# Window attention: the next image's score search interleaved with the second head group, its row transpose moved behind the q/k projection, and the division by the softmax sums cut in eight

## The chip, the cores and the metric

The kernel runs on one core of a Trainium2 chip. The metric is the device time of one execution, in microseconds (us); lower is better. Engine names are those of the profile: PE is TensorE (PEld its weight loads), DVE VectorE, ACT ScalarE, POOL GpSimd, SP the engine that issues the transfers.

## What is computed

Sixteen images of 192 channels and 32 x 32 pixels pass through a convolution layer, an attention layer and two state-space layers. The change touches the attention layer alone. Each pixel of each of 6 heads attends to the 7 x 7 window around it:

```python
qkv = jnp.einsum('bcij,oc->boij', x, w_qkv) + b_qkv[None, :, None, None]
q = qkv[:, :C] * scale
k = qkv[:, C:2 * C]
v = qkv[:, 2 * C:]
kp = jnp.pad(k, ((0, 0), (0, 0), (p, p), (p, p)))
...
for idx in range(win * win):
    dy, dx = (idx // win, idx % win)
    ks = kp[:, :, dy:dy + H, dx:dx + W].reshape(B, heads, dph, H, W)
    scores.append(jnp.einsum('bhdij,bhdij->bhij', qh, ks))
```

A softmax over the 49 positions, the weighted sum of v, an output projection and the residual follow. Keys outside the image are zero but count in the softmax (the "padding terms").

## The kernel before, in words

`attention` (from L1316) handles one image per turn of `main(n)`; the images run in pairs, with images 0 and 1 and the last two written out and a hardware loop of six turns over the pairs between. Turn n finishes image n and prepares image n+1. Each engine has its own `main(n)`, an instruction list in fixed order, and the engines meet only at semaphores.

On PE turn n is: `project` (q, k in three fills, v in four, all of image n+1), `project_out` (output of image n-1, two fills), `pass_b(n, 0)` (scores, then values and sums, of heads 0 to 2 of image n, in 12 pairs of units), `pass_a(n)` (24 pairs of units of image n+1's scores, computed only to find their row maxima), `norm` (group averages for image n+2), `pass_b(n, 1)` (heads 3 to 5), `to_row_layout` (transposes the maxima and padding terms of image n+1, which are then stored to DRAM and loaded back as rows).

All of these but the value sums write to one PSUM tile `work` of two buffers, used strictly in turn: fill k waits until fill k-2 has been drained. A class `Use` counts the fills (59 a turn) and gives each its buffer and number. Who drains: ACT takes q and k (`take_qk`, L1735 and L1737), the rows (`take_rows`, L1777) and the probabilities (`exps`, L1752); DVE takes v (`take_v`, L1853), the maxima (`maxima`, L1872), the averages (`norm_finish`, L1833) and the output (`residual`, L1932).

After each head group ACT copies the sums out (`keep_acc`, L1763 and L1765), and DVE's `divide` takes the reciprocal of the denominators (L1921) and multiplies (L1923). For group 0 of image n that stands on DVE behind the search, for group 1 at the start of turn n+1, ahead of `take_v`. POOL makes the low parts of q and k (`split`, L1995 and L2000). SP stores the three bf16 parts of q and k to DRAM and loads them back in another layout (`move_parts`), stores the output (`store`), and moves the rows (`move_rows`), in this order and waiting for each.

DVE's order in turn n: divide(n-1, 1), take_v, residual, copy_stacks 0, norm_stats, copy_stacks 1, maxima, norm_finish, divide(n, 0), split_padding. `copy_stacks` must be done, and the third q/k part loaded, before the search starts.

Of the kernel before, what the change touches and what calls it, by code (L numbers as in the profile page):

```python
# [10 lines left out]
ALU = mybir.AluOpType  # L11
# [1278 lines left out]
UNIT_PAIRS = 12  # L1290
MASK_ROWS = slice(64, 112)
A_FILLS = 59
# [23 lines left out]
def attention(nc, tag, x_src, x_dst, w, consts, batches):  # L1316
    L, HALF = 1024, 512
    ctx = ExitStack()
    with ctx:
# [93 lines left out]
        def project_use(n, j):  # L1413
            return Use(ZERO, 1 + j) if n is None else Use(n, (34 if n.first else 32) + j)

        def a_use(n, i):
            return Use(ZERO, 8 + i) if n is None else Use(n, 53 + i)

        def norm_use(n):
            return Use(ZERO, 0) if n == "start" else Use(ZERO, 32) if n is None else Use(n, 77)  # L1420

        def rows_use(n):
            return Use(ZERO, 33) if n is None else Use(n, 90 if has(n, 2) else 89)
# [6 lines left out]
        def b_use(n, g, i):  # L1430
            if not has(n, 1):
                return Use(n, (33, 45)[g] + i)
            return Use(n, (41, 78 if has(n, 2) else 77)[g] + i)
# [50 lines left out]
        with nc.Block() as block:  # L1484
            @block.sync
            def _(sp):
# [16 lines left out]
                def move_parts(n):  # L1503
# [3 lines left out]
                    for part, (t, made, k_made, places) in enumerate((  # L1507
                            (qk1, high_made, 3, ((0, q_a, q), (0, k_a, k))),
                            (qk2, mid_made, 1, ((64, q_a, q), (32, k_a, k))),
                            (qk3, low_made, 3, ((32, q_b, q), (0, k_b, k))))):  # L1510
                        if n is not None:
# [3 lines left out]
                        sp.wait_ge(part_stored[part], m.count(16, 16))  # L1515
                        if part == 0 and n is not None and not n.first:

                            sp.wait_ge(group_done, before(n).count(2, 2))
# [5 lines left out]
                def move_rows(n):  # L1524

                    m = after(n)

                    await_all(sp, [(rows_made, m.count(1, 1))] + ([(rows_loaded, m.count(32, 0)), (group_done, m.count(2, 0))]
                                                                  if n is not None else []))
# [13 lines left out]
                def prologue():  # L1543
                    load_residual(ZERO)
                    sp.wait_ge(xn_made, 1)
                    load(Batch(0, 1))
                    move_parts(None)
                    move_rows(None)

                def main(n):  # L1550
# [3 lines left out]
                    if has(n, 1):  # L1554
                        move_parts(n)
# [3 lines left out]
                    if has(n, 1):  # L1559
                        move_rows(n)  # L1560
# [4 lines left out]
            def _(pe):  # L1565
# [8 lines left out]
                def project(n):  # L1574
                    m = after(n)
                    pe.wait_ge(xn_made, m.count(1, 1))
                    for j in range(3):
# [7 lines left out]
                        last.then_inc(filled, 1)  # L1585
                    for j in range(4):
# [25 lines left out]
                def pass_a(n):  # L1612
# [5 lines left out]
                    for i in range(2 * UNIT_PAIRS):  # L1618
                        scores(a_use(n, i), m, i // UNIT_PAIRS, i % UNIT_PAIRS, q_a, q_b, k_a, k_b, 112)

# [20 lines left out]
                def pass_b(n, g):  # L1641
# [6 lines left out]
                    for half in range(2):  # L1648
# [4 lines left out]
                                         skip_group_check=True)  # L1653
                    for i in range(UNIT_PAIRS + 1):
                        if i < UNIT_PAIRS:
                            scores(b_use(n, g, i), n, g, i, k_a, k_b, q_a, q_b, 114)
                        if i:
                            values(n, g, i - 1)
                    nc.tensor.matmul(acc_den[:, 0:1], den_sel[:, 2, :], pad_rows[:, 0:1], start=False, stop=True,
                                     skip_group_check=True).then_inc(group_done, 1)  # L1660
# [5 lines left out]
                def project_out(n_next):  # L1666
                    pe.wait_ge(att_made, n_next.count(2, 0))
# [11 lines left out]
                def to_row_layout(n):  # L1679
                    f = rows_use(n)  # L1680
                    await_unit(pe, f)
                    pe.wait_ge(max_step, after(n).count(5, 5))
# [5 lines left out]
                def prologue():  # L1688
                    norm("start")
                    project(None)  # L1690
                    pass_a(None)
                    norm(None)
                    to_row_layout(None)

                def main(n):
                    if has(n, 1):
                        project(n)
# [16 lines left out]
            def _(act):  # L1714
                def normalise(m):
                    act.wait_ge(norm_step, m.count(7, 7))
                    if not m.first:
                        f = project_use(None if is_static(m, 1) else before(before(m)), 6)
                        await_fill(act, f)
                    for c in range(2):  # L1720
                        last = nc.scalar.activation(image(xn[:, c, :]), x[:, c, :].rearrange("p (y s x) -> p s y x", s=2, x=TILE_W), ACT.Identity,
                                                    scale=rstd[:, c:c + 1], bias=shift[:, c:c + 1])
                    last.then_inc(xn_made, 1)
# [33 lines left out]
                def keep_acc(n, g):  # L1757
# [3 lines left out]
                    if not (n.first and g == 0):  # L1761
                        act.wait_ge(att_made, n.count(2, g))
# [9 lines left out]
                def take_rows(n):  # L1772
                    f = rows_use(n)
                    await_fill(act, f)
                    if n is not None:
                        act.wait_ge(rows_stored, after(n).count(32, 0))
                    nc.scalar.activation(rows_bf[:, :, :], work[0:120, f.unit, :, 0:128], ACT.Copy).then_inc(rows_made, 1)  # L1777
                    act.wait_ge(rows_made, after(n).count(1, 1))
                    act.sem_inc(drained[f.unit], 1)

                def prologue():
                    normalise(ZERO)
# [3 lines left out]
                    normalise(Batch(0, 1))  # L1786
                    take_rows(None)
# [364 lines left out]
```

## Time and profile before

| what | value |
|---|---|
| time, median of 3 runs | 4305.36 us (4305.03 to 4306.83) |
| profiled execution: span from first to last instruction | 4308.6 us |
| profiled execution: device time of its own | not listed beside the span |
| attention layer in the profile | about 380 to 1710 us |
| mean granted TensorE clock | 0.952 |

The profile gives no device time for the profiled execution, so its span stands in for it. The span is 3.2 us (0.08%) above the median of the three timed runs.

In a timeline row the columns are start (us), length (us), engine, line, operation, tiles, count, and in brackets the idle time ahead of it with what ended it.

### The profile page before, as it was taken

Reading aid. Unit: us, or ns where it says so; the run is one execution under the profiler, and the core shown is the slowest. Engines: PE = TensorE matmul, PEld = TensorE weight load, DVE = VectorE, ACT = ScalarE, POOL = GpSimd, SP = SyncE. Lnnn points to the kernel's source line nnn. Section 1 sums busy time; section 2 is a strip of 40 time slices with the busy share of each in tenths; the row PEclk is TensorE's granted clock in tenths of the full one; section 3 lists DMA queues with packets and bytes.
Section 4 is the critical chain, followed back from the end, with each engine's and each line's share of the span. In section 5 each row is a group of like instructions: output and inputs, shape, how many; then the busy total and the mean of one; then the engine's idle time right before and its main releaser. Section 6 shows DMA issues by size and latency. Waiting matters only on the chain.

```text
span 4308.6 us, 119610 instructions
## 1 busy us (share of the span) xinstructions
PE 3710.7 (86%) x49136; PEld 2266.0 (53%) x49136; DVE 3432.3 (80%) x3492; ACT 2105.8 (49%) x2803; POOL 2659.4 (62%) x973
## 2 busy tenths in 40 slices
PE   4994899899999996789889888899898888888897
PEld 4994666666666664344444444444444444444443
DVE  6564567667576663699998998999999989999997
ACT  2331343444444443556555555555565555555563
POOL 1111121111211210599899999999999999999998
PEclk9997899999999998799999999999999999999999
DMA  9624142242332330553543543544535535435433
GB/s 101 85 44 108 54 124 81 85 119 70 95 109 69 105 91 25 120 116 79 125 106 83 125 102 92 125 94 103 122 84 120 112 79 124 109 79 130 103 87 83
DMA packets 296948, 416.40 MB, mean 97 GB/s; under 512 B 31369, under 2 KB 185741, under 8 KB 296385
## 3 DMA queue, kind: packets, MB, share of 16 engines
q1 hardware_dynamic: 295440, 408.35, 41.7%
q8 instruction: 412, 6.75, 0.7%
q14 instruction: 118, 0.97, 0.1%
q10 hardware_dynamic: 978, 0.34, 0.0%
HBM read 267.09 MB, written 91.16 MB: 83 GB/s over the span
## 4 chain that ended last, share of the span: by engine, by line
PE 27%; DVE 16%; issue 12%; ACT 3%; POOL 1%; DVEq 1%; DMA 0%; ACTq 0%; POOLq 0%
DVE ssm_h L1136 11%; PE ssm_u_ps L818 10%; PE ssm_y_ps L831 10%; PE ssm_scratch L848 4%; DVE ssm_b_diag L1160 3%; PE ssm_scratch L858 1%; DVE ssm_stats L1143 1%; POOL ssm_h L1216 1%; ACT ssm_decay L967 1%; PE ssm_u_ps L893 1%; DVE ssm_y_sb L1165 1%; ACT ssm_xn L994 1%; PE ssm_scratch L873 1%; PE ssm_scratch L867 0%; DVEq L1128 0%
## 5 line engine op out<-in xcount | busy, mean ns | idle before, releaser
L1216 POOL TENSOR_TENSOR ssm_h<-ssm_h,ssm_c_rep 128x2048 f32<-128x2048 f32 x384 | 1745.4, 4550 | 107.3 <-DVE ssm_h L1136 99.6
L967 ACT ACTIVATE ssm_decay<-ssm_delta_rep,ssm_a_neg 128x1024 f32<-128x1024 f32 x768 | 863.7, 1145 | 592.1 <-DVE ssm_h L1136 589.3
L818 PE MATMUL ssm_u_ps<-ssm_b_diag,ssm_dx_t 64*64 64x128 f32 x24576 | 865.7, 282 | 262.3 <-DVE ssm_h L1136 182.6
L818 PEld LDWEIGHTS ssm_u_ps<-ssm_b_diag,ssm_dx_t 64*64 64x64 f32 x24576 | 696.3, 137 | 698.9 <-issue 694.6
L1136 DVE TENSOR_TENSOR_SCAN ssm_h<-ssm_decay,ssm_h,ssm_u_ps 128x512 f32<-128x512 f32 x768 | 944.3, 1257 | 132.5 <-PE ssm_u_ps L818 131.4
L1136 DVE TENSOR_TENSOR_SCAN ssm_h<-ssm_decay,ssm_u_ps 128x512 f32<-128x512 f32 x768 | 887.2, 1195 | 35.8 <-ACT ssm_decay L967 16.9
L831 PE MATMUL ssm_y_ps<-ssm_h,ssm_state_sum 128*64 128x512 f32 x3072 | 798.1, 643 | 8.0 <-POOL ssm_h L1216 8.0
L1752 ACT ACTIVATE l_probs<-l_work 128x532 f32<-128x532 f32 (+1 forms) x384 | 217.6, 567 | 560.7 <-PE l_work L1606 554.0
L1160 DVE TENSOR_TENSOR ssm_b_diag<-ssm_b_t,ssm_lane 128x2048 f32<-128x2048 f32 x128 | 454.0, 3549 | 22.7 <-ACT ssm_b_t L1022 22.7
L2004 POOL TENSOR_TENSOR l_rstd<-l_var_eps,l_minus_half 96x2 f32<-96x2 f32 x16 | 11.1, 695 | 586.6 <-DVE l_var_eps L1841 586.6
L831 PEld LDWEIGHTS ssm_y_ps<-ssm_h,ssm_state_sum 128*64 128x64 f32 x3072 | 196.8, 144 | 326.3 <-issue 311.9
L1921 DVE RECIPROCAL l_den<-l_den 96x1024 f32<-96x1024 f32 x32 | 209.6, 6549 | 196.7 <-ACT l_den L1765 196.7
L1995 POOL TENSOR_TENSOR l_qk<-l_qk 128x1024 f32<-128x1024 f32 x48 | 111.6, 2325 | 398.4 <-ACT l_qk L1737 398.4
L1637 PE MATMUL l_acc<-l_probs,l_v 128*32 128x176 f32 (+3 forms) x3072 | 292.8, 275 | 24.5 <-ACT l_probs L1752 20.1
L1637 PE MATMUL l_acc_den<-l_probs,l_ones 128*32 128x176 f32 (+3 forms) x3072 | 291.1, 275 | 0.0
L1236 POOL TENSOR_TENSOR ssm_dx<-ssm_x_kept,ssm_delta 128x256 f32<-128x256 f32 x192 | 254.2, 1343 | 48.7 <-PE ssm_scratch L873 40.1
L1872 DVE TENSOR_REDUCE l_m_raw<-l_work 128x2 f32<-128x532 f32 (+1 forms) x384 | 238.0, 650 | 55.1 <-PE l_work L1606 48.9
L1606 PE MATMUL l_work<-l_k_a,l_q_a 128*128 128x176 bf16 (+3 forms) x1536 | 227.5, 223 | 60.4 <-DVE l_k_a L1863 29.7
L1226 POOL TENSOR_TENSOR ssm_delta<-ssm_relu,ssm_delta 128x512 f32<-128x512 f32 x96 | 249.0, 2594 | 22.7 <-ACT ssm_delta L1009 22.7
L1606 PE MATMUL l_work<-l_q_a,l_k_a 128*128 128x176 bf16 (+3 forms) x1536 | 238.6, 224 | 5.9 <-DVE l_g_mom L1833 5.9
L1637 PEld LDWEIGHTS l_acc<-l_probs,l_v 128*32 128x32 f32 x3072 | 189.6, 111 | 82.7 <-ACT l_probs L1752 30.8
L848 PE MATMUL ssm_scratch<-ssm_xn,ssm_w_delta 97*64 97x512 f32 x768 | 192.7, 624 | 31.7 <-issue 25.8
(163 smaller groups left out, 5554.7 us busy)
## 6 DMA issues: line engine op xcount, KB each, us to landing
ssm_c_rep<-ssm_c_by_state SPq DMA_DIRECT2D x256, 512.0 KB, 6.5
ssm_delta_rep<-ssm_delta SPq DMA_DIRECT2D x384, 128.0 KB, 5.9
l_qk_parts<-l_qk SPq DMA_DIRECT2D x48, 768.0 KB, 4.8
ssm_x<-x_after_l SPq DMA_DIRECT2D x32, 768.0 KB, 5.8
ssm_x_res<-x_after_l SPq DMA_DIRECT2D x192, 128.0 KB, 4.3
l_x<-x SPq DMA_DIRECT2D x64, 192.0 KB, 9.1
x_after_l<-l_x SPq DMA_DIRECT2D x64, 192.0 KB, 4.1
l_x<-x_after_l SPq DMA_DIRECT2D x16, 768.0 KB, 5.5
```

What stands on the lines that cost most here:

```text
L818: made = nc.tensor.matmul(u_ps[64 * par:64 * par + 64, ring("u", w), r, at:at + 128], dx_t[rows, db, 2 * win + k, 64 * g:64 * g + 64], b_d ...
L831: last = nc.tensor.matmul(y_ps[64 * g:64 * g + 64, :], state_sum[:, :], of_half(h[:, s % S_RING, npi, :], g), start=(npq == 0 and npi == 0 ...
L848: last = nc.tensor.matmul(scratch[64 * g:64 * g + 64, :], wt[n.layer][:, ci, 64 * db:64 * db + 64], xn[:, ci, g, :], start=(ci == 0), stop ...
L967: nc.scalar.activation(decay[:, 2 * (s % 2) + npi, :], delta_rep[:, db, :], ACT.Exp, scale=a_neg[:, n.layer, col:col + 1]).then_inc(decay_ ...
L1136: nc.vector.tensor_tensor_scan(h[:, s % S_RING, npi, t], decay[:, 2 * (s % 2) + npi, t], u, start, ALU.mult, ALU.add).then_inc(scanned, 1)
L1160: nc.vector.tensor_tensor(b_diag[:, npq].rearrange("p c a (j i) -> p (c a) j i", i=2), b, m, ALU.mult).then_inc(diag_made, 1)
L1216: nc.gpsimd.tensor_tensor(view, view, c_rep[:, 2 * q:2 * q + 2, :], ALU.mult).then_inc(c_applied, 1)
L1226: nc.gpsimd.tensor_tensor(delta[:, db, :], relu[:, :], delta[:, db, :], ALU.add).then_inc(delta_made, 1)
L1236: made = nc.gpsimd.tensor_tensor(by_lane(dx[:, :], w), in_order(x_kept[:, :], w), in_order(delta[:, db, :], w), ALU.mult)
L1606: last = nc.tensor.matmul(out[:, 0:own] if part == 0 else out[:, own:size], on[m.s][0:r, head, tile_at(TILES[ti])], off[m.s][0:r, head, 51 ...
L1637: last = nc.tensor.matmul(out, by, p, start=False, stop=(i == UNIT_PAIRS - 1), skip_group_check=True)
L1872: nc.vector.tensor_reduce(m_raw[:, 2 * i:2 * i + 2], work[:, f.unit, :, 0:size], AX.X, ALU.max).then_inc(drained[f.unit], 1)
```

## The change

The search fills of image n+1 are put between the score fills of head group 1 of image n on PE, in a list `MIXED`: 8 search fills first, then after each of the 12 group-1 fills one or two more until 24 are done. The averages for image n+2 come before them. On DVE, `maxima` comes after `norm_finish`, and the division of group 0 is cut into eight parts of 128 columns, one after each of the search fills 10 to 17. The division of group 1 is also in eight parts. `norm_stats` moves ahead of `residual`. On ACT the normalisation of image n+2 is split over two places (after exponentials 3 and 7), and the padding terms come after the last exponential. The row transpose of image n+1 moves from the end of turn n to turn n+1, between the q/k and the v projection; ACT takes the rows after q and k; SP moves them after q/k part 0 and ahead of parts 1 and 2.

```diff
+FIRST_SCORES = 8
+MIXED = [("a", i) for i in range(FIRST_SCORES)]
+for _i in range(UNIT_PAIRS):
+    _done = sum(kind == "a" for kind, _ in MIXED)
+    MIXED += [("b", _i)] + [("a", _done + k) for k in range(min(1 + _i % 2, 2 * UNIT_PAIRS - _done))]
+MIXED += [("a", i) for i in range(sum(kind == "a" for kind, _ in MIXED), 2 * UNIT_PAIRS)]
+PARTS = 8
+DIVIDE_AFTER = list(range(10, 10 + PARTS))
...
         def project_use(n, j):
-            return Use(ZERO, 1 + j) if n is None else Use(n, (34 if n.first else 32) + j)
+            return Use(ZERO, 1 + j) if n is None else Use(n, (34 if n.first else 31 if j < 3 else 32) + j)
...
-        def rows_use(n):
-            return Use(ZERO, 33) if n is None else Use(n, 90 if has(n, 2) else 89)
+        def rows_use(m):
+            return Use(ZERO, 33) if m.first else Use(m, 34 if has(m, 1) else 30)
...
# SP, main(n)
                     if has(n, 1):
-                        move_parts(n)
+                        move_parts(n, (0,))
+                    if not n.first:
+                        move_rows(n)
+                    if has(n, 1):
+                        move_parts(n, (1, 2))
                     if not n.first:
                         store(n)
                         load_residual(n)
-                    if has(n, 1):
-                        move_rows(n)
...
# PE
+                def pass_a_and_b(n):
+
+                    await_stacks(n)
+                    for kind, i in MIXED:
+                        if kind == "a":
+                            scores_a(n, i)
+                        else:
+                            if i == 0:
+                                start_group(n, 1)
+                            scores_b(n, 1, i)
+                            if i:
+                                values(n, 1, i - 1)
+                    values(n, 1, UNIT_PAIRS - 1)
+                    end_group()
...
                 def main(n):
                     if has(n, 1):
-                        project(n)
+                        project_qk(n)
+                    if not n.first:
+                        to_row_layout(n)
+                    if has(n, 1):
+                        project_v(n)
                     if not n.first:
                         project_out(n)
                     pass_b(n, 0)
-                    if has(n, 1):
-                        pass_a(n)
                     if has(n, 2):
                         norm(n)
-                    pass_b(n, 1)
                     if has(n, 1):
-                        to_row_layout(n)
+                        pass_a_and_b(n)
+                    else:
+                        pass_b(n, 1)
...
# ACT, main(n)
                     if has(n, 1):
                         take_qk(n)
+                    if not n.first:
+                        take_rows(n)
+                    if has(n, 1):
                         middle_part(n)
...
                         exps(n, 1, i)
-                        if i == 3 and has(n, 1):
-                            padding_terms(n)
-                        if i == 7 and has(n, 2):
-                            normalise(Batch(n.it + 1, n.s))
+                        if i in (3, 7) and has(n, 2):
+                            normalise(Batch(n.it + 1, n.s), i // 4)
+                    if has(n, 1):
+                        padding_terms(n)
                     keep_acc(n, 1)
-                    if has(n, 1):
-                        take_rows(n)
...
# DVE
+                def divide_part(n, g, part):
+                    if part == 0:
+                        dve.wait_ge(acc_kept, n.count(2, g + 1))
+                    cols = slice(part * L // PARTS, (part + 1) * L // PARTS)
+                    nc.vector.reciprocal(den[:, cols], den[:, cols]).then_inc(den_inverted, 1)
+                    dve.wait_ge(den_inverted, n.count(2 * PARTS, PARTS * g + part + 1))
+                    nc.vector.tensor_tensor(att[:, g, cols], att[:, g, cols], den[:, cols], ALU.mult).then_inc(att_made, 1)
...
                         take_v(n)
+                    if has(n, 2):
+                        norm_stats(Batch(n.it + 1, n.s))
                     if not n.first:
                         residual(n)
                     if has(n, 1):
                         copy_stacks(n, 0)
-                    if has(n, 2):
-                        norm_stats(Batch(n.it + 1, n.s))
-                    if has(n, 1):
                         copy_stacks(n, 1)
-                        maxima(n)
                     if has(n, 2):
                         norm_finish(norm_use(n), Batch(n.it + 1, n.s))
-                    divide(n, 0)
                     if has(n, 1):
+                        maxima(n)
                         split_padding(n)
+                    else:
+                        divide(n, 0)
```

## Rows read from the trace of the kernel before

**Rows 1.** The page: span, and busy time of each engine.
```profile
span 4308.6 us, 119610 instructions
```
**Rows 2.** Busy time by stage of one loop turn: start:end, length, busy (count), clock.
```profile
core 0: us, PE busy (x) PEld busy (x) DVE busy (x) ACT busy (x) POOL busy (x), PEclk, DMA share, GB/s
1162.60:1187.80 25.20, 23.26 (x75) 12.37 (x75) 11.41 (x8) 14.12 (x12) 13.28 (x6) 1.00 0.46 132
1187.80:1204.20 16.40, 16.26 (x295) 12.76 (x294) 15.01 (x16) 6.82 (x12) 0.47 (x1) 1.00 0.72 205
1204.20:1240.60 36.40, 32.19 (x488) 26.35 (x487) 25.58 (x47) 13.38 (x19) 0.69 (x1) 0.95 0.06 18
1240.60:1269.20 28.60, 25.00 (x76) 13.09 (x77) 13.32 (x8) 14.12 (x12) 12.24 (x6) 0.94 0.41 117
...
```
**Rows 3.** Who waited for whom, 757.7 to 1550.3 us, ten turns.
```profile
PEld l_work L1606 <- DVE l_m_raw L1872: 31.1, 110, 0.4
```
**Rows 4.** Timeline of PE, first tail.
```profile
1167.34 7.13 PE L1582 MATMUL l_work<-l_xn,l_w_qk 96*128 96x512 f32 x16 [0.85 <-ACTq L1779]
1174.31 1.46 PE L1591 MATMUL l_work<-l_w_v,l_xn 96*128 96x192 f32 x8
1176.87 4.17 PE L1591 MATMUL l_work<-l_w_v,l_xn 96*128 96x192 f32 x24 [1.09 <-ACT l_qk L1737]
1180.87 7.03 PE L1673 MATMUL l_work<-l_att,l_w_o 96*96 96x512 f32 x16
```
**Rows 5.** Timeline of ACT, first tail: the third q/k fill's second copy.
```profile
1175.62 1.20 ACT L1737 ACTIVATE l_qk<-l_work,l_qk_bias,l_qk_scale 128x1024 f32<-128x1024 f32 x1
```
**Rows 6.** Timeline of DVE, first tail.
```profile
1166.87 6.55 DVE L1921 RECIPROCAL l_den<-l_den 96x1024 f32<-96x1024 f32 x1 [10.09 <-ACT l_den L1765]
1173.45 1.22 DVE L1923 TENSOR_TENSOR l_att<-l_att,l_den 96x1024 f32<-96x1024 f32 x1
1175.81 0.56 DVE L1853 TENSOR_TENSOR l_v<-l_work,l_b_v 128x384 f32<-128x384 f32 x1 [1.14 <-PE l_work L1591]
```
**Rows 7.** Timelines of PE, POOL and DVE, second tail.
```profile
1243.57 12.26 PE L1582 MATMUL l_work<-l_xn,l_w_qk 96*128 96x512 f32 x24 [2.51 <-issue]
...
1251.38 2.12 POOL L1995 TENSOR_TENSOR l_qk<-l_qk 128x1024 f32<-128x1024 f32 x1 [26.97 <-ACT l_qk L1737]
...
1251.45 3.13 DVE L1923 TENSOR_TENSOR l_att<-l_att,l_den 96x1024 f32<-96x1024 f32 x1
```
**Rows 8.** Timeline of PE: first matmuls of two following search fills.
```profile
1204.19 0.25 PE L1606 MATMUL l_work<-l_k_a,l_q_a 128*128 128x176 bf16 x1
...
1204.62 0.24 PE L1606 MATMUL l_work<-l_k_a,l_q_a 128*128 128x176 bf16 x1
```
**Rows 9.** Timeline of DVE: search, and the end of norm_finish.
```profile
1204.81 1.09 DVE L1872 TENSOR_REDUCE l_m_raw<-l_work 128x2 f32<-128x418 f32 x2 [1.52 <-PE l_work L1606]
...
1211.70 5.15 DVE L1872 TENSOR_REDUCE l_m_raw<-l_work 128x2 f32<-128x532 f32 x8 [0.16 <-PE l_work L1606]
...
1224.52 0.16 DVE L1843 SCALAR_TENSOR_TENSOR l_shift<-l_g_mom,l_rstd 96x2 f32<-96x2 f32 x1 [0.88 <-POOL l_rstd L2004]
```
**Rows 10.** Timeline of PE, group 1: its longest wait.
```profile
1235.86 0.38 PE L1637 MATMUL l_acc<-l_probs,l_v 128*32 128x224 f32 x1 [1.41 <-ACT l_probs L1752]
```
**Rows 11.** Two stretches on either side of the start of group 1.
```profile
1220.10:1223.50 3.40, 2.69 (x29) 1.81 (x27) 3.03 (x16) 0.52 (x1) 0.00 (x0) 1.00 0.00 0
1223.50:1226.90 3.40, 3.40 (x52) 2.80 (x50) 2.52 (x3) 1.04 (x2) 0.69 (x1) 0.50 0.00 0
```
**Rows 12.** Timeline of SP's queue, first tail: issues.
```profile
1167.62 1.54 SPq L1531 DMA_DIRECT2D l_max_rows<-l_rows_bf  x2
1170.58 0.26 SPq L1535 DMA_DIRECT2D l_q_b<-l_max_rows  x1
...
1175.74 0.39 SPq L1514 DMA_DIRECT2D l_qk_parts<-l_qk  x1
1179.35 0.80 SPq L1522 DMA_DIRECT2D l_q_a<-l_qk_parts  x2
```

More of the change, by code:

```diff
@@ L1432, in b_use @@
                 return Use(n, (33, 45)[g] + i)
[L1433 removed]
+            return Use(n, 41 + i) if g == 0 else mixed_use(n, "b", i)
         def await_unit(pe, f):
@@ L1510, in move_parts @@
                             (qk3, low_made, 3, ((32, q_b, q), (0, k_b, k))))):
+                        if part not in which:
+                            continue
                         if n is not None:
@@ L1514, in move_parts @@
                         sp.dma_start(qk_dram[part].rearrange("(t p) c -> p t c", p=128), t[:, :, :]).then_inc(part_stored[part], 16)
-                        sp.wait_ge(part_stored[part], m.count(16, 16))
-                        if part == 0 and n is not None and not n.first:
-                            sp.wait_ge(group_done, before(n).count(2, 2))
+                        await_all(sp, [(part_stored[part], m.count(16, 16))]
+                                  + ([(group_done, before(n).count(2, 2))] if part == 0 and n is not None and not n.first else []))
                         for base, out, side in places:
@@ L1617, in pass_a, with scores_a, scores_b @@
                     pe.wait_ge(part_loaded[2], m.count(64, 64))
-                    for i in range(2 * UNIT_PAIRS):
-                        scores(a_use(n, i), m, i // UNIT_PAIRS, i % UNIT_PAIRS, q_a, q_b, k_a, k_b, 112)
+                def scores_a(n, i):
+                    scores(a_use(n, i), after(n), i // UNIT_PAIRS, i % UNIT_PAIRS, q_a, q_b, k_a, k_b, 112)
+                def scores_b(n, g, i):
+                    scores(b_use(n, g, i), n, g, i, k_a, k_b, q_a, q_b, 114)
                 def values(n, g, i):
@@ L1714, in _, with normalise @@
             def _(act):
[L1715 to L1723, printed above, removed]
+                def normalise(m, c):
+                    if c == 0:
+                        act.wait_ge(norm_step, m.count(7, 7))
+                        if not m.first:
+                            f = project_use(None if is_static(m, 1) else before(before(m)), 6)
+                            await_fill(act, f)
+                    done = nc.scalar.activation(image(xn[:, c, :]), x[:, c, :].rearrange("p (y s x) -> p s y x", s=2, x=TILE_W), ACT.Identity,
+                                                scale=rstd[:, c:c + 1], bias=shift[:, c:c + 1])
+                    if c:
+                        done.then_inc(xn_made, 1)
                 def take_qk(n):
@@ L1873, in maxima @@
                                                 AX.X, ALU.max).then_inc(drained[f.unit], 1)
+                        if n is not None and i in DIVIDE_AFTER:
+                            divide_part(n, 0, DIVIDE_AFTER.index(i))
                     for i in (2 * UNIT_PAIRS - 2, 2 * UNIT_PAIRS - 1):
@@ L1886, in maxima @@
                     if n is not None:
-                        await_fill(dve, rows_use(None if n.first else before(n)))
+                        await_fill(dve, rows_use(n))
                     nc.vector.tensor_scalar(m_hi[:], m_max[:], -1.0, None, ALU.mult).then_inc(max_step, 1)
```

77 lines of the change are left out of this document (43 added, 34 removed).

## The prediction

> **What bounds the kernel now.** I read the page, then busy time by stage, then the waits, then the timelines of one loop turn. The profiled execution spans 4308.6 us [rows 1], 3.2 us above the median of the timed runs, 4305.4; I work out a difference in the trace and add it to the median. A difference under 0.2% (8.6 us) can't be told from none.
>
> One loop turn holds two images and lasts 159.4 us. Per image there are three stages [rows 2]: the tail (projections), 25.2 us in one image, 28.6 us in the other; head group 0, about 16.4; search and group 1, 36.4 (36.8 in the other). PE is busy nearly throughout each, DVE, ACT and POOL are not, so the path is PE's list with its waits. What waits there are: the search, paced by DVE (a large part of PE's idling there ends with DVE's maxima [rows 3]); 1.41 us in group 1 behind ACT's normalisation [rows 10]; 0.85 and 1.09 us in the first tail [rows 4]; 2.51 us at the loop's branch in the second [rows 7]. After the averages and the start of group 1 the granted clock falls from 1.00 to 0.50 (2.4 to 1.2 GHz) for 3.4 us [rows 11].
>
> **The mixed pass (15 times).** Count from the end of group 0. PE's own work: a small search fill is 0.43 us (1204.19 to 1204.62 [rows 8]), a large one, with 532 columns for 418, about 0.55, so 24 are 11.8; group 1 costs what group 0 does, 16.4; the averages 0.4. Sum 28.6 us, the floor. DVE's: norm_finish about 1.8, most of it small steps and a wait for POOL [rows 9]; maxima 0.55 small (1.09 for two) and 0.64 to 0.67 large (5.15 for eight) [rows 9], 24 of them 14.6; eight divisions. A part's reciprocal is an eighth of 6.55 [rows 6], 0.82, to which comes at most 0.16, the length of DVE's smallest operation [rows 9]; its multiply an eighth of 1.22, 0.15, plus the same. So 0.97 to 1.29 a part; I take 1.16, near the upper end because each multiply waits for its reciprocal. Eight are 9.3, DVE's sum 25.7. Both fit in 29, but PE can be only two fills ahead, so the order decides:
>
> - Averages, then search fills 0 and 1 by 1.3. Fill 2 waits for maxima 0, which stands behind norm_finish: 2.3 + 0.55. The first eight are then at DVE's pace; PE ends fill 7 at 6.5, where its own work was 4.2.
> - Start of group 1 (four small matmuls, 1.0), group fills 0 and 1, search fills 8, 9, 10: DVE takes up maxima 10 at about 11.1, waiting for nobody long.
> - Maxima 10 to 17 with a division part behind each: 2 x 0.67 + 6 x 0.55 + 9.3 = 13.9 on DVE, to 25.0. PE in this stretch has some 8 x 0.46 + 5.3 x 1.2 = 10. DVE sets the pace and PE loses nearly 4.
> - Search fill 18 ends at 24.6. Left on PE: five large search fills 2.75, four score fills 2.4, value sums 7 to 11 3.6, and a tenth of a us at each of a dozen waits for a buffer, 1.2: to 34.6.
>
> 34.6 against 36.5 before: 1.9 gained, 15 times, 28.5. Bounds: 28.6 (nothing waits, -7.9) and 37 (every buffer wait twice as long, +0.5). The rest of DVE's chain, 1.5 us for the last maxima, ends about with group 1, so ACT's padding terms do not hold keep_acc up. Normalising in two pieces costs nothing, because other fills lie between; uncovered it would be the 1.41 of before.
>
> **The tail.** Before, q/k fill 1 waited for ACT's rows. That wait of 0.85 goes. But the third q/k fill and the first v fill now share a buffer (the rows' fill stands between). Before, the first v fill followed at once (1174.31) and ran while ACT took q/k [rows 4]; now it waits until ACT is done, 2.3 us after the fill (before, 1174.5 to 1176.82 [rows 5]).
>
> - First kind of tail (7 times): q/k fills end at 3.6, 7.1, 10.5; ACT is done with them at 12.85; v fills end at 14.1, 15.4, 16.7, 18.0; the output projection, 7.0, ends at 25.0. So 0.2 gained at best.
> - DVE's divide, though, is ahead of take_v. Before, the one multiply came once: 1.22 beside nothing, 3.13 when POOL's L1995 had started 0.07 before it, that is, it ended 1.08 after POOL's did [rows 6, 7]. Eight multiplies now spread over 9 us that hold three POOL operations of 2.12, at about 6.6, 9.5 and 12.9 (each as ACT finishes a fill). With a part each 1.16 from 4.25 (the first reciprocal's start before, 1166.87, less 1162.6 [rows 6]), multiplies 2, 3 and 5 fall into them and wait for their ends, 8.7, 11.6 and 15.0. Divide ends at 17.5 instead of 12.1. The first v fill has been ready since 14.1, the third needs its buffer: v ends at 20.7, output projection at 27.6: 2.4 later than before.
> - Second kind (7 times): the branch, 2.5, and PE's slow first fill at half clock put q/k's end at 15.2 as before; ACT frees the buffer at 17.5, four v fills 5.2, output 7.0: 29.7 against 28.6, 1.1 lost. Divide is done by 16.5 and in time.
>
> The Trainium skill, page "SBUF — State Buffer", section on the engines' ports, says this as a rule: the port pair that VectorE and GpSimd share is an exclusive lock held for a whole instruction, and a VectorE operation with two SBUF inputs blocks on it. By that rule, the trace agrees: 3.13 for 1.22. Without the rule the first tail would gain 0.2 and not lose 2.4.
>
> Tails: 7 x 2.4 + 7 x 1.1 = 24.5 lost.
>
> **Other edits.** Rows: SP issues them behind part 0. Part 0's store to its loads is 3.6 (1175.74 to 1179.35), the row stores to the row loads 3.0 [rows 12]. From the third q/k copy (11.7 in the first kind) store 3.7, load issue 1.8, row stores 3.0 to 5, behind the loads' bytes: row loads at 20.2 to 22.2, landed perhaps 2 later, needed at 27.6 (29.7, and all 4.8 later, in the second kind: just in time). Parts 1 and 2 come about 1 us later than before or none, since they start 5 earlier and let the rows by; they are needed at the end of group 0, about 44. norm_stats moves into the time in which DVE waits for the output projection's first fill (3.5, half of 7.0 [rows 4], after the last take_v), and costs nothing; without that cover its length, under 3.5, would come on top. The load of the next x no longer stands behind the rows on SP, which gives it only more time. At image 15 and at the very end divide is on the path and in parts: 2 x 1.5 (9.3 for 6.55 and 1.22) = 3.
>
> Clock. In the first tail PE now waits 2.0 and 2.6 within 8 us, where it waited 0.85 and 1.09 and kept 1.00. The branch's 2.5 alone brought 0.50. I take one stretch of 3.4 at half clock, 1.7 lost, 7 times: 12. The mixed pass drops too, but mostly under DVE's pace: 0.3 x 15 = 4 net. Bounds 0 and 40.
>
> Sum: -28.5 + 24.5 + 3 + 16 = +15, so 4320.
>
> **Rivals.**
> (a) Faster: DVE keeps up. Parts at the lower end, maxima at 0.55, so the mixed pass takes 32 (gain 4.5 x 15 = 67); multiplies still meet POOL (+24.5, +3). 4305.4 - 40 = 4265. For it: DVE has 9 us of slack over the pass. Against: two buffers. 0.34.
> (b) Cancelled: as forecast, with no multiply blocked for long and no new clock falls: -28.5 + 6 + 3 + some clock, 4290 to 4312; I take 4305. 0.14.
> (c) Slower by late rows: if the row stores wait for all of part 0's loads and the row loads land over 2 us later than reckoned, group 0 starts late, 2 us 14 times on top: 4348. It decides once rows land more than 25 us after q/k part 0 could be issued in the second kind of tail. 0.10.
>
> **How the numbers follow.** Forecast 0.42 (own range 4300 to 4340), (a) 0.34, (b) 0.14, (c) 0.10. Range 4260 to 4346. Faster by over 0.2%: (a) and a little of (b), 0.36. Within: most of (b) and the lower edge of the forecast, 0.22. Slower: 0.42.
>
> **What would show it.** Right: group 0's end to group 1's end near 34.6; DVE without gaps through maxima 10 to 17; multiplies of 128 columns with one in three near 1 to 2 us; first v fill waiting 2 us for L1737; take_v late in the first kind; clock 0.50 in tails. Wrong: a mixed pass near 31 with PE busy throughout (then a), or PE's first matmul of group 0 released by the row loads (then c).

## The result, and the profile after

The changed kernel takes 4367.3 us (median of 4 runs) against 4306.1 for the kernel before, measured beside it: a ratio of 1.0143 (95% interval 1.0127 to 1.0159), slower by some 61 us. The forecast was slower, 4320, with 4346 as the upper end: the sign was right, the size was not. The profiled execution spans 4365.5 us, 56.9 more than before. One of the four executions of e2_v_first, below, took 19082 us, which nothing here explains, and its ratio leaves that one out.

Busy time by stage in the changed kernel, one loop turn's worth but for one group 0 (columns as in [rows 2]): the start of the mixed pass (up to group 1's first fill), the rest of it, the first kind of tail, group 0, a whole mixed pass, the second kind of tail.

```profile
span 4365.5 us, 120316 instructions
...
1163.60:1171.10 7.50, 5.73 (x67) 5.05 (x67) 4.87 (x12) 4.07 (x4) 0.69 (x1) 0.77 0.34 94
1171.10:1199.40 28.30, 24.92 (x425) 20.69 (x422) 21.01 (x43) 9.31 (x15) 0.00 (x0) 1.00 0.12 30
1199.40:1229.50 30.10, 27.93 (x75) 17.20 (x74) 20.46 (x36) 14.17 (x13) 12.66 (x6) 0.83 0.36 108
1229.50:1245.90 16.40, 16.26 (x295) 12.77 (x294) 11.91 (x8) 6.82 (x12) 0.00 (x0) 1.00 0.67 197
1245.90:1281.50 35.60, 30.44 (x488) 25.62 (x487) 25.88 (x55) 13.38 (x18) 0.69 (x1) 0.95 0.09 24
1281.50:1314.50 33.00, 27.80 (x76) 15.30 (x76) 18.97 (x37) 14.17 (x13) 12.66 (x6) 0.84 0.26 78
```

Against [rows 2]: mixed pass 35.8 and 35.6 for 36.4 twice (the 36.8 of the prediction has 0.4 us of the row transpose in it), group 0 unchanged, tails 30.1 for 25.2 and 33.0 for 28.6.

The turn of [rows 2] is not like every other, though. A mixed pass of the kernel before takes 35.0 us where the clock stays at 1.00 and 36.4 where it falls for 3.4 us, and that turn has two of the second sort. A pass of each kernel without a fall, before and changed:

```profile
1127.60:1162.60 35.00, 30.80 (x488) 25.36 (x487) 25.56 (x47) 13.38 (x19) 0.69 (x1) 1.00 0.06 13
831.10:865.80 34.70, 29.36 (x489) 24.71 (x488) 25.70 (x55) 13.39 (x19) 0.69 (x1) 1.00 0.12 29
```

So I add up every stage of the profiled executions, with the same bounds. The fifteen tails go from 393.9 to 460.7 us, 66.8 more. The fifteen mixed passes go from 540.8 to 539.9, 0.9 less: nearly nothing is gained. Group 0 is 16.4 us in all sixteen images of both. Outside these stages the changed kernel's execution is 9 us shorter, with 18 us less at half clock, in code that the change leaves nearly as it was. Together that is the 56.9 between the two spans. The loss is in the tails.

The clock column says more. Time at half clock in a stage is twice (1 - clock) times its length: in the first tail 2 x 0.17 x 30.1 = 10.2 us, where it was none; in the second 2 x 0.16 x 33.0 = 10.6, where it was 3.4. Half of such time is lost where PE is busy: the v fills below take 10.41 us at 0.50, and 5.36 in e10, where the clock is 1.00. Over all tails it grows from some 37 to some 150 us, over all mixed passes from 37 to 65.

The first tail in the changed kernel. PE:

```profile
1199.36 10.57 PE L1593 MATMUL l_work<-l_xn,l_w_qk 96*128 96x512 f32 x24
1209.76 0.38 PE L1722 MATMUL l_work<-l_ident,l_to_rows 128*120 128x128 f32 x2
1212.32 10.41 PE L1604 MATMUL l_work<-l_w_v,l_xn 96*128 96x192 f32 x32 [2.17 <-ACT l_qk L1782]
1222.56 7.03 PE L1711 MATMUL l_work<-l_att,l_w_o 96*96 96x512 f32 x16
```

DVE (division, then take_v at L1901) and, last, POOL (three rows):

```profile
1206.06 0.94 DVE L1973 RECIPROCAL l_den<-l_den 96x128 f32<-96x128 f32 x1
1207.04 1.29 DVE L1975 TENSOR_TENSOR l_att<-l_att,l_den 96x128 f32<-96x128 f32 x1
1208.26 0.94 DVE L1973 RECIPROCAL l_den<-l_den 96x128 f32<-96x128 f32 x1
1209.23 1.95 DVE L1975 TENSOR_TENSOR l_att<-l_att,l_den 96x128 f32<-96x128 f32 x1
...
1213.26 1.34 DVE L1975 TENSOR_TENSOR l_att<-l_att,l_den 96x128 f32<-96x128 f32 x1
...
1216.69 0.29 DVE L1975 TENSOR_TENSOR l_att<-l_att,l_den 96x128 f32<-96x128 f32 x1
1216.90 0.55 DVE L1901 TENSOR_TENSOR l_v<-l_work,l_b_v 128x384 f32<-128x384 f32 x1
...
1206.06 2.12 POOL L2051 TENSOR_TENSOR l_qk<-l_qk 128x1024 f32<-128x1024 f32 x1 [40.55 <-ACT l_qk L1782]
1208.91 2.12 POOL L2051 TENSOR_TENSOR l_qk<-l_qk 128x1024 f32<-128x1024 f32 x1 [0.72 <-ACT l_qk L1782]
1212.34 2.12 POOL L2051 TENSOR_TENSOR l_qk<-l_qk 128x1024 f32<-128x1024 f32 x1 [1.31 <-ACT l_qk L1782]
```

A multiply of 128 columns takes 0.29 alone. The three that start while POOL computes take 1.29, 1.95 and 1.34, and each ends 0.15 after POOL's operation does. They are multiplies 2, 3 and 5, counted from 0. The division ends 17.6 us after group 1 (1216.98 less 1199.4). PE waited 2.17 for ACT ahead of the v fills, as foreseen, and then the v fills took 10.4 us, because the clock was at 0.50 (1.2 GHz) throughout. The third of them was ready for its buffer just as take_v let it go: the late division shows as a wait of 0.20 and no more, because the two fills ahead of it took twice their time.

```profile
1217.50 4.93 PEld L1604 LDWEIGHTS l_work<-l_w_v,l_xn 96*128 96x128 f32 x16 [0.20 <-DVE l_v L1901]
...
1213.00:1222.00 9.00, 9.00 (x30) 8.80 (x29) 5.46 (x9) 2.77 (x1) 6.04 (x4) 0.50 0.50 146
```

### The profile page after: what moved, and what is told of

The parts are those of the page before. It is cut to its first block, busy times and chain, and to the rows that moved or that the text cites. A ratio compares the mean times of both kernels' runs of the same rounds, so it can differ in the third digit from the quotient of the medians.

```text
span 4365.5 us, 120316 instructions
## 1 busy us (share of the span) xinstructions
PE 3737.6 (86%) x49136; PEld 2306.5 (53%) x49136; DVE 3511.5 (80%) x3940; ACT 2108.8 (48%) x2803; POOL 2648.5 (61%) x973
## 4 chain that ended last, share of the span: by engine, by line
PE 24%; DVE 16%; issue 12%; ACT 5%; POOL 1%; DVEq 1%; DMA 0%; ACTq 0%; POOLq 0%
DVE ssm_h L1136 11%; PE ssm_u_ps L818 9%; PE ssm_y_ps L831 9%; PE ssm_scratch L848 3%; DVE ssm_b_diag L1160 3%; ACT ssm_decay L967 2%; ACT ssm_xn L994 1%; PE ssm_scratch L858 1%; DVE ssm_stats L1143 1%; POOL ssm_h L1216 1%; DVE ssm_y_sb L1165 1%; PE ssm_scratch L873 1%; PE ssm_u_ps L893 1%; ACT ssm_delta L1007 0%; PE ssm_scratch L867 0%
## 5 line engine op out<-in xcount | busy, mean ns | idle before, releaser
L2051 POOL TENSOR_TENSOR l_qk<-l_qk 128x1024 f32<-128x1024 f32 x48 | 101.9, 2123 | 658.4 <-ACT l_qk L1782 658.4
L1973 DVE RECIPROCAL l_den<-l_den 96x128 f32<-96x128 f32 x256 | 240.6, 940 | 76.1 <-ACT l_den L1810 76.1
```

## The experiments

L is the theory that small multiplies behind POOL make the division late; B, that the buffer shared by the third q/k fill and the first v fill is what costs; C, that PE's waits cost twice, themselves and by a lower clock after them. Tails are given as first kind, second kind. The runs come from several chips, so where two are close I go by their ratios to the kernel before, measured beside each.

**e1_tail_whole**: group 1's division whole again.

```diff
                 def divide(n, g):
-                    for part in range(PARTS):
-                        divide_part(n, g, part)
+                    if g == 0:
+                        for part in range(PARTS):
+                            divide_part(n, g, part)
+                        return
+                    dve.wait_ge(acc_kept, n.count(2, g + 1))
+                    nc.vector.reciprocal(den[:, :], den[:, :]).then_inc(den_inverted, PARTS)
+                    dve.wait_ge(den_inverted, n.count(2 * PARTS, PARTS * g + PARTS))
+                    nc.vector.tensor_tensor(att[:, g, :], att[:, g, :], den[:, :], ALU.mult).then_inc(att_made, PARTS)
```

> The changed kernel with the division of group 1 whole again (one reciprocal, one multiply), that of group 0 still in eight. Theory L (multiplies wait for POOL, the division ends late and take_v with it, and the waits that follow pull the clock down): the first kind of tail, 30.2 us in the changed kernel, falls to 26.5 to 27, its stretch at half clock from 10.2 to 3.4 us; the second kind stays at 33.0. Time 4367 - 7 x 3.4 = 4343. Rival B (only the buffer shared by the third q/k fill and the first v fill matters): both tails stay, time 4360 to 4370.

Measured: 4329.2 us, ratio to before 1.0044 (1.0027 to 1.0061), 38 less than the changed kernel and under the 4343 expected. The tails, and the first one's v fills:

```profile
1179.10:1206.00 26.90, 24.73 (x76) 14.18 (x76) 16.39 (x22) 14.16 (x13) 12.66 (x6) 0.94 0.31 93
1096.60:1124.50 27.90, 23.05 (x75) 12.51 (x74) 16.95 (x22) 14.16 (x13) 12.65 (x6) 1.00 0.29 88
...
1192.03 7.15 PE L1604 MATMUL l_work<-l_w_v,l_xn 96*128 96x192 f32 x32 [2.17 <-ACT l_qk L1782]
```

The first tail fell as L said, and its half clock from 10.2 to 3.2 us, though PE's wait of 2.17 is still there. The second fell too, from 33.0 to 27.9, which L didn't foresee: PE waits there nearly as before (2.68 at the branch, 2.17 ahead of the v fills), but the clock stayed at 1.00. That is so in three of the five tails behind the branch; the others took 32.9 and 31.6. And part of the gain goes elsewhere: the mixed pass after such a tail has 10 us at half clock and takes 38.0, every second one 34.7, so that the fifteen passes together are as long as in the changed kernel.

```profile
1141.10:1179.10 38.00, 33.27 (x489) 27.23 (x488) 25.98 (x55) 13.35 (x18) 0.69 (x1) 0.87 0.18 43
```

So a wait of that length doesn't always bring the clock down, and a fall that one stage is spared can come in a later one. What decides it these runs don't tell.

**e2_v_first**: the first v fill ahead of the row transpose (and `Use` numbers to match).

```diff
                         project_qk(n)
+                        project_v(n, (0,))
                     if not n.first:
                         to_row_layout(n)
                     if has(n, 1):
-                        project_v(n)
+                        project_v(n, (1, 2, 3))
```

> The changed kernel with the first v fill ahead of the row transpose, so that it no longer shares the buffer of the third q/k fill; division still in parts. Theory B (shared buffer): PE's wait of 2.17 us before the v fills goes to about 1 us in both kinds, no half clock after it; second kind of tail 33.0 to 30, first kind to 27. Time about 4325. Theory L: in the first kind the second v fill now waits for take_v behind the late division, so that tail stays at 29 to 31 and only the second falls. Time about 4345.

Measured: 4374.4 us, 1.0152 (1.0132 to 1.0172), not to be told from the changed kernel's 1.0143; both theories expected less. Tails 31.0 to 33.3 and 27.5 to 30.3. In a first one:

```profile
1040.17 0.43 PE L1722 MATMUL l_work<-l_ident,l_to_rows 128*120 128x128 f32 x2 [1.17 <-ACT l_qk L1783]
1045.28 7.33 PE L1604 MATMUL l_work<-l_w_v,l_xn 96*128 96x192 f32 x24 [4.68 <-DVE l_v L1902]
```

The wait for ACT is 1.17 now, but PE then waits 4.68 for take_v, which stands behind the division, and goes on at half clock. B is right about the wait and wrong about the time: with the division late the shared buffer was only the first of two doors. The second tail gained some 3, the first lost 1 to 3, and group 0 took 17.3 to 20.2 in five of the sixteen images, which is taken up next.

**e3_both**: e1's and e2's edits together.

> Both edits together: group 1's division whole and the first v fill ahead of the rows. If late division and shared buffer are together the cause of the tails' growth, the tails come to 25 (first kind) and 29 to 30 (second kind; before the change 25.2 and 28.6), the mixed pass stays at 35.8, time 4300 to 4310. If the clock falls for another reason (the mixed pass), the tails stay above 28 and 32.

Measured: 4317.8 us, 1.0025 (1.0013 to 1.0036), above the 4300 to 4310 expected. Tails 24.2 and 27.1 to 30.4: together they are back at the tails of before, the first even shorter. But group 0 is 17.5 to 18.9 instead of 16.4 in thirteen images, and most mixed passes take 34.7 and 38.0 by turns, as in e1. DVE in the tail, and POOL beside it:

```profile
1276.39 0.28 DVE L1871 BATCH_NORM_AGGREGATE l_moments<-l_stats 96x2 f32<-96x12 f32 x2 [0.16 <-DVE l_stats L1866]
1276.70 3.56 DVE L1875 SCALAR_TENSOR_TENSOR l_moments<-l_moments 96x1 f32<-96x1 f32 x2
1280.19 2.71 DVE L1995 SCALAR_TENSOR_TENSOR l_x_res<-l_work,l_b_o,l_x_res 96x512 f32<-96x512 f32 x4
...
1273.96 6.29 POOL L2063 TENSOR_TENSOR l_qk<-l_qk 128x1024 bf16<-128x1024 f32 x3 [2.96 <-ACT l_qk L1788]
```

Two operations on one column each, 0.34 us in the changed kernel's first tail, take 3.56 and end with POOL's last. They belong to norm_stats, which the change had moved ahead of residual, into the time of POOL's L2063. Residual is late, and group 0's first fills wait for it (0.52 and 0.74), with 3.4 us at half clock behind.

**e5_stats_back**: as e3_both, norm_stats behind residual and the first copy_stacks.

```diff
-                    if has(n, 2):
-                        norm_stats(Batch(n.it + 1, n.s))
                     if not n.first:
                         residual(n)
                     if has(n, 1):
                         copy_stacks(n, 0)
+                    if has(n, 2):
+                        norm_stats(Batch(n.it + 1, n.s))
+                    if has(n, 1):
                         copy_stacks(n, 1)
```

> As e3_both, and norm_stats behind residual and the first copy_stacks again, as before the change. In e3_both group 0 takes 18.8 us instead of 16.3; in it DVE's two one-column operations of norm_stats (L1875) take 3.56 us while POOL's L2063 runs, and residual, the first two score fills of group 0 and then a half-clock stretch follow. Theory L: group 0 is back at 16.3 in every image, so 15 x 2.5 = 37 off e3_both's 4318: 4280 to 4290, faster than the kernel before. Rival (group 0 is long because the rows arrive late): group 0 stays at 18.8, time 4315 to 4320.

Measured: 4295.1 us, 0.9966 (0.9956 to 0.9976): faster than the kernel before. Group 0 is back at 16.4 in every image, as L said. The time is 5 above the range expected; the runs spread from 4283.5 to 4305.6, and the profiled one is the fastest of them. Its stages (most of its mixed passes take 34.7 at a clock of 1.00; the one shown is one of three with a fall):

```profile
1142.80:1167.00 24.20, 23.03 (x75) 12.45 (x74) 12.78 (x14) 14.27 (x13) 12.53 (x6) 1.00 0.29 87
1167.00:1183.40 16.40, 16.26 (x295) 12.79 (x294) 15.00 (x16) 6.79 (x12) 0.12 (x1) 1.00 0.63 187
1183.40:1218.80 35.40, 30.59 (x488) 25.84 (x487) 25.87 (x55) 13.35 (x18) 0.69 (x1) 0.95 0.22 61
```

**e6_before_parts**: the kernel before, only its divisions in eight parts.

```diff
-                    nc.vector.reciprocal(den[:, :], den[:, :]).then_inc(den_inverted, 1)
-                    dve.wait_ge(den_inverted, n.count(2, g + 1))
-                    nc.vector.tensor_tensor(att[:, g, :], att[:, g, :], den[:, :], ALU.mult).then_inc(att_made, 1)
+                    for part in range(PARTS):
+                        cols = slice(part * L // PARTS, (part + 1) * L // PARTS)
+                        nc.vector.reciprocal(den[:, cols], den[:, cols]).then_inc(den_inverted, 1)
+                        dve.wait_ge(den_inverted, n.count(2 * PARTS, PARTS * g + part + 1))
+                        nc.vector.tensor_tensor(att[:, g, cols], att[:, g, cols], den[:, cols], ALU.mult).then_inc(att_made, 1)
```

> The kernel before with nothing changed but both divisions in eight parts. Theory L: in the first kind of tail multiplies fall into POOL's operations, take_v and the projection are late: 25.3 us becomes 27 to 29; in the second kind (28.7) the division ends before v is ready, or one us late: 28.7 to 30. The parts behind the search are off PE's path (group 1 hides them). Time 4308 + 7 x 3 = 4320 to 4340. Rival (parts cost only in company with the shared buffer): tails 25.3 and 28.7 as before, time 4306 to 4312.

Measured: 4362.6 us, 1.0127 (1.0106 to 1.0147), above the 4320 to 4340 expected. This one edit makes the kernel before almost as slow as the whole change does. The two tails, and PE and DVE in the first:

```profile
1187.30:1217.90 30.60, 26.15 (x75) 14.91 (x74) 16.65 (x22) 14.12 (x12) 12.72 (x6) 0.89 0.54 158
1269.30:1299.60 30.30, 26.66 (x76) 13.69 (x75) 13.87 (x22) 14.12 (x12) 12.28 (x6) 0.89 0.38 111
...
1205.63 5.47 PE L1592 MATMUL l_work<-l_w_v,l_xn 96*128 96x192 f32 x16 [2.43 <-DVE l_v L1854]
...
1198.30 2.19 DVE L1926 TENSOR_TENSOR l_att<-l_att,l_den 96x128 f32<-96x128 f32 x1
```

First tail 30.6 for 25.2, of it 2.43 by PE's wait for take_v; the rest comes with a clock of 0.89, that is 6.7 us at half. In the second the division ends in time and PE waits as in the kernel before (2.54 at the branch, 1.09 ahead of the v fills); all that differs is the clock, 6.7 us at half for 3.4, and why the small multiplies bring that these runs don't show. Two of the five such tails of the kernel before have it as well. The expectation had the mechanism and the wait, and was short of the clock's share, as the prediction was.

**e9_one_multiply**: the changed kernel, group 1's eight reciprocals first, then one multiply (group 0 keeps its parts).

```diff
+                    for part in range(PARTS):
+                        cols = slice(part * L // PARTS, (part + 1) * L // PARTS)
+                        nc.vector.reciprocal(den[:, cols], den[:, cols]).then_inc(den_inverted, 1)
+                    dve.wait_ge(den_inverted, n.count(2 * PARTS, PARTS * g + PARTS))
+                    nc.vector.tensor_tensor(att[:, g, :], att[:, g, :], den[:, :], ALU.mult).then_inc(att_made, PARTS)
```

> The changed kernel with group 1's eight reciprocals kept, but behind them one multiply of 1024 columns. Theory L (small multiplies standing behind POOL): the reciprocals are not held by POOL and end some 7.6 us after the first, the multiply falls between two POOL operations, the division ends 13.2 us after group 1's end instead of 17.5; first kind of tail 30.3 to about 27, as with the division whole (e1_tail_whole, 27.0); time 4325 to 4345. Rival (the parts' own overhead, 1.6 us, is what makes the division late): tail near 30, time 4360 to 4370.

Measured: 4323.8 us, 1.0047 (1.0030 to 1.0064), where 4325 to 4345 was expected for L; first tail 27.0 in the image that starts at 1004.6, mostly 28.3 to 28.6 in others of its kind.

```profile
1009.01 6.63 DVE L1985 RECIPROCAL l_den<-l_den 96x128 f32<-96x128 f32 x8 [2.93 <-ACT l_den L1810]
1015.75 1.69 DVE L1987 TENSOR_TENSOR l_att<-l_att,l_den 96x1024 f32<-96x1024 f32 x1
```

The rival, overhead of the parts, falls: eight reciprocals on end cost 6.63, one of full width 6.55 [rows 6], and the time is that of e1. It is the small multiplies between them.

**e4_filler** and **e10_whole_filler**: three more matmuls of 512 columns ahead of the row transpose (in the trace 2.6 us of work), in the changed kernel and in e1_tail_whole. Their result is not used.

```diff
+                    if not m.first and has(m, 1):
+                        for c in range(3):
+                            nc.tensor.matmul(work[:, f.unit, 1, :], w_qk[:, c % 2, 0:128], xn[:, c % 2, 0:HALF], start=True, stop=True)
```

> The changed kernel with three more 512-column f32 matmuls (0.59 us each) ahead of the row transpose, into the transpose's own buffer, overwritten or unread: they fill most of PE's wait of 2.17 us before the v fills and compute nothing that is used. Theory C (it is the fall of the clock after that wait that costs, beside the wait itself): more work on PE, yet shorter: the stretch at half clock in the second kind of tail after that wait goes, 33.0 to 31.3; the first kind still has the late division, 30.2 to 27.5 or 28.5. Time 4335 to 4350. Rival: the half clock has nothing to do with that wait; the time stays at 4367 or rises by up to 2.

> e1_tail_whole with three more 512-column matmuls ahead of the row transpose, as in e4_filler; their result is not used. In e1_tail_whole nothing but the shared buffer holds PE in the first kind of tail (2.17 us), yet the v fills behind it take 7.1 us instead of 5.5: half clock. Theory C: with most of that wait filled the clock stays at 1.00, the tail goes from 27.0 to 25.3, time 12 below e1_tail_whole's 4329: 4310 to 4320. Rival (the half clock comes from elsewhere): tail 27.0 or more, time 4329 or more.

Measured: e4_filler 4350.8 us, 1.0095 (1.0078 to 1.0112), tails 29.5 and 31.2; e10_whole_filler 4313.3 us, 1.0015 (1.0003 to 1.0026), tails 25.4 and 29.8 to 31.5; e4 is just above its 4350, e10 within its 4310 to 4320. By the medians each is 16 us less than the kernel that it adds work to. For e4 that is beyond doubt; e10's interval only just clears e1's (1.0027 to 1.0061), and its profiled execution is the fastest of ten. The first tail of e10, stage and v fills, and the v fills of a first tail of e4:

```profile
1157.50:1182.90 25.40, 25.40 (x82) 13.64 (x83) 17.51 (x23) 14.28 (x13) 12.66 (x6) 1.00 0.32 99
...
1170.72 5.36 PE L1604 MATMUL l_work<-l_w_v,l_xn 96*128 96x192 f32 x32
...
1196.93 2.77 PE L1604 MATMUL l_work<-l_w_v,l_xn 96*128 96x192 f32 x16
1201.87 4.55 PE L1604 MATMUL l_work<-l_w_v,l_xn 96*128 96x192 f32 x16 [2.18 <-DVE l_v L1904]
```

In e10 PE never pauses, the clock is 1.00, and the v fills take 5.36 where e1's took 7.15. That is C, for this tail. In e4 the first two v fills run at full clock, and now PE stands before the late division: the wait of 2.18 for take_v that the half clock hid in the changed kernel. The tails behind the branch, 29.8 to 31.5 in e10 for 28.0 to 32.9 in e1, are not shorter: a fall that these runs show and don't explain.

**e7_spread**, **e11_norm_late_only** and **e8_norm_late** go on from e5_stats_back. In e7 the division parts of group 0 follow every second search fill; in e11 the averages and norm_finish follow the first eight; e8 has both. Of the edits below the first is that of e7, the other two are those of e11 (what they remove is left out).

```diff
-DIVIDE_AFTER = list(range(10, 10 + PARTS))
+DIVIDE_AFTER = list(range(8, 8 + 2 * PARTS, 2))
...
                             if i == 0:
+                                if has(n, 2):
+                                    norm(n)
                                 start_group(n, 1)
...
+                        if n is not None and has(n, 2) and i == FIRST_SCORES - 1:
+                            norm_finish(norm_use(n), Batch(n.it + 1, n.s))
```

> As e5_stats_back, with group 0's division parts after every second search fill from 8 to 22, not after each from 10 to 17. Theory D (the run of eight maxima with a part behind each holds PE up by some 4 us in the mixed pass): from group 1's start to its end 28.2 becomes 24.5 to 25.5; 15 x 3 = 45 off e5_stats_back, about 4240. Rival (the pass is bound by PE and by its waits for the two buffers): 27.5 to 28.2, time within 10 of e5_stats_back.

> As e7_spread, with the averages and norm_finish behind the first eight search fills instead of ahead of them. PE then does not wait for norm_finish at the pass's start: from group 0's end to group 1's start 6.5 to 7.5 becomes 6.0, and the half clock that follows that start in some images goes. 1 us x 15: about 4225. Rival (norm_finish only moves its wait behind the eight fills): within 5 of e7_spread.

> e5_stats_back with the averages and norm_finish behind the first eight search fills; group 0's parts back at search fills 10 to 17. It tells which of e8_norm_late's two edits gave its 20 us. If the place of norm_finish alone: group 0's end to group 1's start 5.7 instead of 6.5 to 7.5, time 4270 to 4280. If it needs the spread parts as well: 4290 or more.

Measured: e7 4291.1 us, 0.9958 (0.9944 to 0.9972); e11 4280.0, 0.9942 (0.9926 to 0.9959); e8 4273.1, 0.9914 (0.9897 to 0.9931). Group 1's part of the mixed pass is 28.3 in e5 and 27.8 in e7, far from theory D's 25, and e7's time can't be told from e5's; nor is e8 near the 4225 expected. Theory D falls: that the eight parts stand behind one maximum after the other was not what held PE. PE waits for DVE's maxima eight times there, 3.1 us in all, in e5 and in the changed kernel, and still seven times, 2.8 us, in e7; that each part holds a drain up wherever it stands is my reading, not tested. The pass's start is 5.6 to 5.8 in nearly all images of e11 and e8 for 6.4 to 7.4, as expected of norm_finish, and e11 came out at its expected 4270 to 4280. One turn's stages of e8, first tail, group 0, mixed pass, second tail:

```profile
1138.30:1162.60 24.30, 23.14 (x78) 12.52 (x77) 12.82 (x15) 14.27 (x13) 12.56 (x6) 1.00 0.28 86
1162.60:1178.90 16.30, 16.16 (x294) 12.71 (x293) 15.00 (x16) 6.79 (x12) 0.10 (x1) 1.00 0.70 203
1178.90:1213.40 34.50, 30.57 (x488) 25.61 (x488) 25.95 (x55) 13.34 (x18) 0.69 (x1) 0.95 0.20 56
1213.40:1242.10 28.70, 24.82 (x77) 13.09 (x77) 13.95 (x15) 14.27 (x13) 12.48 (x6) 0.94 0.26 76
```

e8 beats both kernels: the mix as intended, group 0's parts spread, group 1's division whole, the first v fill ahead of the rows, norm_stats where it was, norm_finish later.

## Why the prediction was right and wrong

**Right: the lock on the small multiplies.** Foretold: multiplies 2, 3 and 5 wait for POOL's ends and the division ends at 17.5. Found: those three, and 17.6. e1, e6 and e9 show it as the largest single cause, 38 us when taken out of the changed kernel and some 54 when put alone into the kernel before, each with the clock that it brings. The Trainium skill, page "SBUF — State Buffer", section "Who interferes with whom", has the port pair that VectorE shares with GpSimd as an exclusive lock for a whole instruction, and says that a VectorE operation with two SBUF inputs meets it against a GpSimd operation that reads SBUF. The trace agrees for the multiplies (up to 1.95 and 2.19 for 0.29) and for the one-column operations of norm_stats (3.56 for 0.34), and the reciprocals, with one input, were 0.94 beside POOL as without it.

**Right: the shared buffer.** PE's wait of about 2 ahead of the v fills was 2.17, in both kinds of tail.

**Wrong: the clock.** The step that failed is the last term, "I take one stretch of 3.4 at half clock, 1.7 lost, 7 times: 12", with 4 more in the mixed pass: 16 us, bounds 0 and 40. It took one fall in one kind of tail. Found were 10.2 us at half clock in nearly every tail. Over all tails the time at half clock grew by 113 us and over the mixed passes by 27, so up to 70 us were lost by it, most of them, 56, in the tails. That alone is 54 us more than the term. Take the 70 away and what is left of the stages is -4 us, near the -1 that the prediction's other terms add up to (-28.5 + 24.5 + 3). e10 shows the cause from the other side: with the wait filled by useless work, the same fills ran at 1.00.

What the clock did to the first tail is worth a second look. The prediction added a wait of 2.6 for take_v and a stretch of 3.4 at half clock, 29.3 in all; 30.1 was found, close by luck. The wait for take_v all but vanished (0.20), because the fills ahead of it ran at half clock, and the half clock lasted 10.2. With that clock mended by the filler, the wait came back (2.18 in e4). The second kind was to take 29.7 and took 33.0, and (10.6 - 3.4) / 2 = 3.6 is the clock's. It comes five times and the first kind nine, not seven each, as the loop branches back five times; that changes the 24.5 by under 3.

**Wrong: the mixed pass's gain.** Foretold were 1.9 us a pass and 28.5 in all, found 0.9 in all. The new pass was foretold well: 34.6, and 34.7 found where the clock stays up. Its start took 7.5 for 6.5, with a clock of 0.77, 3.4 us at half; from there on 28.1 was foretold and 28.3 found. What was wrong is the pass that it was compared with. 36.5 is the pass of the kernel before with a fall of the clock in it, 35.0 the one without, so the order itself gives 0.3 and not 1.9. In the kernel before seven passes take 36.3 to 36.7 and six 34.9 to 35.1; in the changed one nine take 35.5 to 35.8, three 37.9 to 38.0. Read a baseline from more than one turn. Of the reasons given inside the pass, "maxima 10 to 17" set DVE's pace (13.9 foretold, 13.8 found, without gaps), PE waited 3.1 for DVE in the whole of this part, and the wait of 1.41 behind ACT's normalisation is gone; but spreading the parts gave 0.5 and not the 4 that they were to cost. What is left of PE's waits there (24.9 busy of 28.3) is not settled beyond that; the two buffers in strict turn remain the likely reason, not tried.

**Wrong: norm_stats "costs nothing".** Its move was named as covered by DVE's wait for the projection. In the changed kernel's first tail it is, since the projection is late itself: POOL's run ends at 1223.71 and the two operations start at 1226.17 (group 0 16.4). In e3, where the projection is on time, it cost 2.5 us of group 0, by the same lock that the prediction had used two paragraphs earlier for the multiplies and not for these.

**Rivals.** The late rows didn't come: row loads were issued at 1220.75 for a group 0 at 1229.5. The mix that DVE keeps up with (a) did not come: its pass of 32 us was never reached. e8, with five more edits, is at 4273 near its 4265 by luck: its passes, mostly 33.4 to 34.6, gain less than (a) says, and its tails lose nothing, where (a) has the same loss as the forecast.

## What to carry to other kernels

Before a vector operation is cut into pieces or moved, list what GpSimd does at that time: a two-input piece, however small, can wait for a whole GpSimd operation, and eight pieces have eight chances. Price a new wait of TensorE by the work at half clock behind it as well: behind the wait of 2.17 it was 1.7 us lost in e1's first tail, 5.1 in the changed kernel's. When an edit looks useless alone (e2 gained nothing, e1 38, both together 50), look for a second wait right behind the first. And count the passes with and without a fall of the clock before one of them is taken as the baseline.

## What was not expected of the hardware

Adding 2.6 us of useless matmuls per image made two kernels 16 us faster. Nearly equal waits of TensorE (2.7 to 3.0 and 2.17 in the second tail) were followed by 10.6 us at half clock in the changed kernel and by none in e1_tail_whole, where the next mixed pass had them instead. Eight reciprocals of 128 columns on end took 6.63 us, 0.83 each, but 0.98 each from start to multiply when one followed each.
